# Attention with a row maximum: the turn of the next unit's queries moved behind the first sums and the row fill of its tile

## The reference

```python
x = x + tanh(g_xattn[l]) * xattn_l(layernorm(x), context, ...)
# in each xattn:
q, k, v = heads(x @ Wq + bq), heads(context @ Wk + bk), heads(context @ Wv + bv)
scores = einsum('bhid,bhjd->bhij', q, k) * scale      # masked
attn = softmax(scores, axis=-1)                        # exp(s - rowmax) / sum
out = einsum('bhij,bhjd->bhid', attn, v) @ Wo + bo
```

## Time and profile before

| | us |
|---|---|
| median of 3 runs | 8040.48 (8039.37 to 8040.94) |
| the profiled execution | 8037.15 |
| its span | 8035.4 |
| TensorE / VectorE / ScalarE busy | 5948.6 / 6533.6 / 5210.8 |
| L1034 reduces, all 2496 | 2739.8 |
| L999 exponentials, all 4896 | 2649.4 |

### The profile page before, as it was taken

One profiled execution on the slowest core, in us unless ns is written; L12 is line 12 of the kernel. 1 busy time (PEld: TensorE's weight loads), 2 busy tenths in 40 slices (PEclk: granted clock), 3 DMA queues, 4 the chain that ended last, 5 costly groups with the idle time before them and its releaser, 6 DMA issues. The chain is left out here.

```text
span 8035.4 us, 123712 instructions
## 1 busy us (share of the span) xinstructions
PE 5948.6 (74%) x45093; PEld 1946.0 (24%) x45093; DVE 6533.6 (81%) x11562; ACT 5210.8 (65%) x8393; POOL 755.1 (9%) x394
## 2 busy tenths in 40 slices
PE   5699997499997455534555777767888875899987
PEld 2122222122222111101110111134444442222223
DVE  5999972699992899999997999966656665999934
ACT  3399995089997455424545999954555551699992
POOL 2000000000000000000000000054435540000000
PEclk8699999699998555555557999988989996899998
DMA  7100001300000000000002000000000002000001
GB/s 220 40 16 5 18 2 48 73 4 18 17 3 4 22 8 8 13 4 8 8 4 50 17 17 3 1 30 14 9 14 11 9 9 59 3 17 18 3 2 48
DMA packets 112345, 176.36 MB, mean 22 GB/s; under 512 B 14817, under 2 KB 94725, under 8 KB 106750
## 3 DMA queue, kind: packets, MB, share of 16 engines
q1 hardware_dynamic: 111774, 168.91, 8.3%
HBM read 125.66 MB, written 43.21 MB: 21 GB/s over the span
## 5 line engine op out<-in xcount | busy, mean ns | idle before, releaser
L1034 DVE TENSOR_REDUCE a_partial<-a_row 128x2 f32<-128x988 f32 x2496 | 2739.8, 1179 | 130.7 <-PE a_row L908 127.6
L999 ACT ACTIVATE a_prob<-a_score 128x512 f32<-128x512 f32 x4896 | 2649.4, 595 | 110.8 <-PE a_score L921 98.4
L934 PE MATMUL a_acc<-a_prob,a_v_all 128*9 128x256 f32 x19584 | 1526.1, 384 | 0.6 <-ACT a_prob L999 0.6
L517 ACT COPY m_rows<-m_score 128x1536 f32<-128x1536 f32 (+1 forms) x640 | 760.9, 1250 | 847.2 <-DVE m_edge L568 691.4
L908 PE MATMUL a_row<-a_kg,a_qn 54*128 54x494 bf16 x4992 | 1030.9, 410 | 272.1 <-DVE a_partial L1034 212.6
L576 DVE MAX8 m_cand<-m_rows 128x8 f32<-128x192 f32 x4352 | 1213.8, 332 | 13.6 <-ACT m_rows L517 13.6
L496 PE MATMUL m_score<-m_kb,m_qb 54*128 54x512 bf16 (+1 forms) x1664 | 766.3, 608 | 415.3 <-ACT m_rows L517 349.4
L921 PE MATMUL a_score<-a_qb,a_kg 54*128 54x512 bf16 x4896 | 939.4, 380 | 70.8 <-ACT a_prob L999 25.7
L798 DVE SCALAR_TENSOR_TENSOR a_prob<-a_score,a_prob 128x1024 f32<-128x1024 f32 x816 | 925.0, 1216 | 37.9 <-ACT a_prob L774 37.9
L774 ACT ACTIVATE a_prob<-a_score,a_lower 128x1024 f32<-128x1024 f32 x816 | 865.9, 1111 | 84.6 <-PE a_score L715 34.1
L908 PEld LDWEIGHTS a_row<-a_kg,a_qn 54*128 54x128 bf16 x4992 | 243.6, 94 | 1386.8 <-DVE a_partial L1034 1228.9
(11 more groups left out here) (305 smaller groups left out, 5692.5 us busy)
## 6 DMA issues: line engine op xcount, KB each, us to landing
kst<-kv_parts SPq DMA_DIRECT2D x48, 384.0 KB, 3.9
a_kg<-kst SPq DMA_DIRECT2D x60, 306.0 KB
vst<-kv_va SPq DMA_DIRECT2D x48, 288.0 KB, 4.1
e_cb<-comb SPq DMA_DIRECT2D x25, 512.0 KB
a_kg<-kst SPq DMA_DIRECT2D x60, 204.0 KB
a_v_all<-vst SPq DMA_DIRECT2D x3, 3672.0 KB
qst<-q_parts SPq DMA_DIRECT2D x24, 256.0 KB
a_kg<-kst SPq DMA_DIRECT2D x60, 102.0 KB
```

Of the source, the lines that this page charges most:

```text
L517: act.copy(rows[i][:, c * CH:c * CH + n], score[(i * NCH + c) % 2][:, 0:n]).then_inc(copied, 1)
L934: last = pe.matmul(acc[32 * j:32 * j + VW, columns], v_all[:, k, u // NQC * G + j, :], prob[tile % PROBS][:, j // 2, j % 2, columns], star ...
L999: act.activation(prob[tile % PROBS][:, j // 2, j % 2, :], score[use % 3][:, :], ACT.Exp).then_inc(slot_out, 1)
L1034: dve.tensor_reduce(partial[:, u % 2, 2 * item:2 * item + 2, c], row[use % 2][:, :, 0:CW], AX, ALU.max).then_inc(reduced, 1)
```

## The change

The two lines that call the turn stand behind `sums(tile - 1, 0)` and the first row fill of the tile, instead of ahead of them. They stay ahead of the next tile's first scores. Nothing else differs: the same instructions with the same waits, on every engine but TensorE in the same order.

```diff
                 scores(tile, 1)
-                if k == TURN_AT and u + 1 < UNITS:
-                    turn(u + 1)
                 if k == HEADS_AT and u:
                     heads(u - 1)
                 pairs = row_pairs(tile)
                 if tile:
                     sums(tile - 1, 0)
                 row_fills(tile, pairs[:1])
+                if k == TURN_AT and u + 1 < UNITS:
+                    turn(u + 1)
                 if tile + 1 < UNITS * KT:
                     scores(tile + 1, 0)
                 if tile:
                     sums(tile - 1, 1)
                 row_fills(tile, pairs[1:])
```

## The result

The changed kernel takes 8014.2 us (median of 7 runs, 8010.5 to 8017.1) against 8040.9 for the kernel before (7 runs, 8039.4 to 8045.4) on the same chip: a ratio of 0.9966, with a 95% interval of 0.9955 to 0.9978. The forecast was 8015.5. The profiled execution is 8014.2 with a span of 8012.4, 23.0 us shorter than before.

A forecast was written before the change was run, and what follows sets the result against it. VectorE's row search was taken to pace the unit, waiting on TensorE's order at the turn. Gains of 22.9, 1.7 and 0.3 us, together 24.9, gave 8015.5 us from a median of 8040.48; range 8006 to 8031.

The forecast's parts named there:

- (a): Ahead of the turn: moved sums and fill fit TensorE's 0.78 us idle time, free within a cover of 0.06 us.
- a turn released by VectorE instead of ScalarE: At the turn: listed as a sign that the forecast is wrong; the turn's release by ScalarE was to remain.
- (b): First reduce after the turn's start: at +0.67 us without wait, before +3.37 at half clock, +1.95 at full clock.
- (c): Second reduce after the turn's start: at +2.71 us, before +4.47 at half clock, +3.05 at full clock.
- (d): ScalarE's exponentials after the turn's start: at +1.83 us, before +2.15 and +3.58, staying in step with VectorE.
- (e): TensorE's granted clock at the turns: taken as 1.00 at all 18, the other bound being 0.55 at the same 13.
- (f): 7th turns, where only sums move: scores come forward from +1.52 to +1.42 us, 0.1 us each.
- The sum: Gain over all turns: 22.9 us at 13, 1.7 at 5, 0.3 at the 7th turns, together 24.9 us.
- The first, slower one: At the turn: the moved fill holds TensorE until a reduce ends, about 0.6 us at 18 turns; 8051 us, chance 0.03.
- The second, that the clock still falls: At the turns: gain only 9 to 12 us, 8030 us, or 8023 if half fall; chance 0.15 for most or half.
- The third, given back at the unit's boundary: At the unit's boundary: VectorE runs ahead and waits longer there, so the time stays at 8040 us; chance 0.04.

The follow-up runs named there:

- zeros in the second wait: Kernel before, plus three matmuls of zeros in TensorE's 0.78 us wait between the scores and the turn: 8023.5 us, ratio 0.9980.
- late fill behind the turn: Changed kernel, with the tile's second row fill moved from behind the next scores and sums to right behind the turn: 8017.4 us, ratio 0.9972.

## Why the prediction was right

**Cause.** It said that TensorE waits ahead of ready work at the turn, and that VectorE, which paces the unit, pays. Moving the work brought 26 us. Two things are narrower than it said: 17 to 19 of these come by way of the clock, and of the two pieces moved only the sums were needed.

**(a) The cover.** It was smaller than read. I took 0.22 us from a fill to the next matmul, as from fill to scores. From a fill to a turn matmul it is 445.20 - 444.89 = 0.31. So the turn is not released by ScalarE any more but follows the fill, and starts 1.19 us after the scores, not 1.15. The fill in its turn goes 0.06 after the end of a reduce, at all 18 turns, as in the kernel with the fill alone ahead, where the same distances show VectorE ending a wait of 0.49 us. One of the prediction's signs of being wrong, a turn released by VectorE instead of ScalarE, thus came true. It cost little: the prediction had named the cover of 0.06 us and the price beyond it, as much as the turn is late, and that is 0.04 us a turn. The cover was missed, and that it was missed by so little is luck.

**(b), (c), (d).** The first reduce has no wait. Its place before, +3.37 "in the 13 turns", was read from one of them; they range from +2.59 to +3.39. The sum doesn't use it. It uses the second reduce, +4.47, whose mean over the 13 is 4.50. In the changed kernel this second reduce stands at +2.64 (+2.59 at the first turns), forecast +2.71. The scores came 0.06 after the copy's end and not 0.14 (446.49, with the end at 445.85 + 0.59 = 446.44), so they stand at +1.35 at most turns, 0.07 earlier than forecast, counted from a turn that starts 0.04 late. The two nearly cancel. The exponentials stand at 446.92, +1.72, and at +1.77 in most turns, forecast +1.83.

**(e) The clock.** The largest term, and the only one that had to be chosen between two ends. It held at 1.00 in all 18 turns. When it was forecast no row showed the 1.20 us wait without the 0.78; the kernel with zeros in the second wait does. The zeros alone, by the median, brought 17 us of the 18.5 that 13 x 1.42 had given for them. The Trainium skill's page "TensorE: Matmul & The Clock Gate" (section "A second HAM failure mode: psum-queue depth-cycling") has short idle times between groups of matmuls make the clock oscillate; the runs agree, with 13 falls from two waits of 1.20 and 0.78 us, and none when either is filled. The long idle stretches against which that page's section "Why this matters for your kernels" warns are not needed for a fall here.

**(f)** The 7th turns' scores stand 1.33 after the turn's start, forecast 1.42, 1.52 before: 0.2 us each instead of 0.1.

**The sum.** From the turns' distances, the 13 steps behind low-clock turns brought 24.0 us (1.84 each, forecast 1.76), the 5 others 1.9 (0.38, forecast 0.34), the 7th turns 0.6, together 26.5, where the sum had 24.9. Off this go 1.1 us at 7698.67, below. The span shrank by 23.0. The rest, 2.4 us, was lost on balance where the change touches nothing: 2.0 us were gained ahead of the first turn (329.49 us to 331.54 before), 0.5 lost in small pieces, and 3.9 lost in the stretch from the end of layer 1's attention to the first turn of layer 3's, 4326.5 us to 4322.6 before (windows of both traces, start:end, length, busy of each engine):

```profile
2545.20:6871.70 4326.50, 2732.11 (x14645) 1007.80 (x14645) 3615.87 (x8525) 2368.77 (x3189) 709.18 (x345) 0.74 0.06 15
```
```profile
2564.70:6887.30 4322.60, 2725.86 (x14645) 1004.50 (x14645) 3615.55 (x8525) 2370.67 (x3189) 709.61 (x345) 0.74 0.06 15
```

The instructions are the same, and 4 us there lie within the scatter of the runs (8010.5 to 8017.1). Why this stretch varies was not tested. That the median came out within 1.3 us of the forecast is thus partly luck: the turns gained 1.6 us more than the sum, and the scatter elsewhere is larger than both.

**The rivals.** The first, slower one was right in its mechanism. The fill does hold the turn in this kernel, but by the 0.04 us, and not by a whole reduce. The kernel with both fills ahead waits a whole reduce and shows the price, 1.1 us a turn where the rival had 1.03; its 8051 took the clock as low too, and 8040 was measured. The second, that the clock still falls, came true in other kernels: at 8 turns with the fill only ahead (8035, forecast for this rival 8030) and at 4 with both fills ahead. The third, given back at the unit's boundary, is out: VectorE's waits there are 0.43 and 0.15 us before and after.

## What to carry to other kernels

On an engine that works in order, look for work that is ready behind an instruction that waits, and price it by the next engine's wait, not by the idle time itself. Then ask which instruction is late next: of two moved pieces one brought everything, and the tile's other fill, moved ahead of the turn as well, took the whole gain back. Where TensorE has two short waits close together, look at the granted clock: filling either may be worth more than the waits themselves.

## What the runs showed of the hardware

Useless matmuls in a short wait of TensorE can pay: three of 128 by 512, in a wait of 0.78 us, gave 17 us back over 18 turns, by the clock alone.

How often the clock fell at the 18 turns goes with the waits of TensorE ahead of the turn. With 1.20 and 0.78 us it was 13, with 1.20 and 0.49 it was 8, and with 1.20 and 0.22 none. With the 1.20 alone it was none of 54, in three kernels (changed, late fill behind the turn, zeros in the second wait). With the 0.78 whole and 0.39 left of the 1.20 it was none. With both fills ahead, where 0.71 us stand further behind the 1.20, it was 4. These are counts of one execution each.

A single wait of 1.2 us can be enough for the clock to fall, if rarely. In the last unit of layer 3's attention, behind the copy of the sums, the changed kernel's clock fell once (timeline, then window with the clock in the third-last column):

```profile
7698.67 0.60 PE L921 MATMUL a_score<-a_qb,a_kg 54*128 54x512 bf16 x2 [1.21 <-ACT a_prob L999]
```
```profile
7698.70:7702.20 3.50, 3.50 (x22) 0.53 (x22) 0.00 (x0) 2.58 (x5) 0.00 (x0) 0.51 0.00 0
```

The same wait, of 1.21 us, left it full in the same place of layers 0 and 1. It is in all nine kernels, three times in each profiled execution. The clock fell at 2 of these 27, the other in layer 1 of the kernel with zeros in the second wait. Each fall made the last unit 1.1 to 1.3 us longer. No row is filled in this place. So a wait's length alone doesn't tell whether the clock falls. The 1.20 us before the turn, alone, never took it down in the 54 turns above, but a forecast can't count on that from its length.
